# Deformable convolution with a gathered neighbour table: the table built from normalised rows that TensorE turns, as interleaved row pairs

## The reference, cut to what matters

```python
x = x + _L0_conv_ref(_gn(x), offset_w, offset_b, conv_w)      # _gn: group norm, (v - mean) / sqrt(var + eps)

def _L0_conv_ref(x, offset_w, offset_b, conv_w):
    offset = conv2d(x, offset_w) + offset_b                   # 9 taps, 2 coordinates each
    xp = pad(x, 1)                                            # zeros around the normalised image
    p = p0 + pn + offset                                      # where each tap of each pixel samples
    q = floor(p)
    ...
    g_lt = (1 - (py - qlt_y)) * trunc(1 - (px - qlt_x))
    g_rb = (1 - (qrb_y - py)) * trunc(1 - (qrb_x - px))
    g_lb = (1 - (py - qlt_y)) * (1 - (qrb_x - px))
    g_rt = (1 - (qrb_y - py)) * (1 - (px - qlt_x))
    x_off = g_lt * xp[qlt_y, qlt_x] + g_rb * xp[qrb_y, qrb_x] + g_lb * xp[qlt_y, qrb_x] + g_rt * xp[qrb_y, qlt_x]
    return conv2d(x_off, conv_w, stride 3)                    # the 9 samples of a pixel by the 9 taps
```

## Time and profile before

| | |
|---|---|
| median of 3 runs | 3207.58 us (3206.52 to 3216.11) |
| profiled execution | 3214.02 us, its span 3212.2 us |
| TensorE busy | 2880.1 us, 90% |
| VectorE busy | 1898.5 us, 59% |
| ScalarE busy | 1828.8 us, 57% |
| GpSimd busy | 1764.4 us, 55% |
| granted TensorE clock, mean | 0.957 of full speed |
| moved by DMA | 405.97 MB |

### The profile page before, as it was taken

The page is one execution under the profiler, slowest core; times in us unless marked ns, Lnnn a source line. Parts: engine busy times, 40 slices in busy tenths (PEclk is TensorE's granted clock), DMA queues, the critical chain, the costliest instruction groups (busy, mean ns, idle before and its releaser), DMA issues. The chain is left out here.

```text
span 3212.2 us, 53916 instructions
## 1 busy us (share of the span) xinstructions
PE 2880.1 (90%) x19490; PEld 2195.3 (68%) x19490; DVE 1898.5 (59%) x7142; ACT 1828.8 (57%) x4004; POOL 1764.4 (55%) x1815
## 2 busy tenths in 40 slices
PE   4588999999999999999999999999999998999555
PEld 2466776777777777677777776777767776777432
DVE  1456664766576664766477664766486657564324
ACT  1355665666566665666566665666566666664220
POOL 1777764775467654775467644765477556710000
PEclk9699999999999999999999999999999999999787
DMA  5634333552255333643255333633255324411397
GB/s 148 200 112 129 116 112 108 144 139 86 87 153 154 94 96 105 159 119 104 88 136 154 94 90 110 170 110 102 84 148 158 89 81 110 117 66 43 118 341 282
DMA packets 265861, 405.97 MB, mean 126 GB/s; under 512 B 44681, under 2 KB 175977, under 8 KB 265083
## 3 DMA queue, kind: packets, MB, share of 16 engines
q0 software_dynamic: 86400, 236.04, 26.4%
q1 hardware_dynamic: 175323, 153.11, 15.7%
q10 hardware_dynamic: 3872, 13.37, 1.0%
HBM read 368.42 MB, written 85.35 MB: 141 GB/s over the span
## 5 line engine op out<-in xcount | busy, mean ns | idle before, releaser
L495 POOL DMA_INDIRECT shared<-pair_table,idx x1800 | 1752.2, 973 | 1061.5 <-issue 524.6
L1041 PE MATMUL bank_o<-vals,prob_t 128*128 128x128 f32 x5200 | 701.0, 280 | 50.5 <-ACT prob_t L531 49.0
L531 ACT ACTIVATE prob_t<-bank_r 128x512 f32<-128x512 f32 (+3 forms) x728 | 394.9, 547 | 609.6 <-PE bank_r L1028 607.4
L751 DVE CUSTOM_DVE_ANT_0 prob<-bank_s,mask 128x512 f32<-128x512 f32 (+3 forms) x728 | 453.8, 631 | 456.9 <-PE bank_s L1019 453.5
L1041 PEld LDWEIGHTS bank_o<-vals,prob_t 128*128 128x128 f32 x5200 | 637.4, 193 | 84.1 <-ACT prob_t L531 73.7
L1019 PE MATMUL bank_s<-keys,qt 128*128 128x512 f32 (+3 forms) x1456 | 661.4, 560 | 17.4 <-DVE cmax L751 17.4
L518 ACT ACTIVATE shared<-shared,wa 128x128 f32<-128x128 f32 x1800 | 564.2, 390 | 75.9 <-DMA shared<-pair_table,idx 75.9
L741 DVE SCALAR_TENSOR_TENSOR shared<-shared,wb 128x128 f32<-128x128 f32 x1800 | 502.3, 346 | 118.1 <-ACT shared L518 117.4
L1005 PEld LDWEIGHTS bank_conv<-convw_t,smp_t 128*128 128x128 f32 x3600 | 460.1, 200 | 97.8 <-ACT smp_t L524 56.7
L1005 PE MATMUL bank_conv<-convw_t,smp_t 128*128 128x128 f32 x3600 | 497.2, 286 | 32.3 <-ACT smp_t L524 32.2
L1028 PE MATMUL bank_r<-ident,prob 128*128 128x128 f32 x2600 | 417.3, 279 | 1.8 <-ACT prob L598 1.8
(11 more groups left out here) (155 smaller groups left out, 2315.2 us busy)
## 6 DMA issues: line engine op xcount, KB each, us to landing
pair_table<-in_dram SPq DMA_DIRECT2D x224, 224.0 KB
shared<-in_dram SPq DMA_DIRECT2D x32, 1024.0 KB, 9.2
shared<-pair_table,idx POOLq DMA_INDIRECT x1800
shared<-in_dram SPq DMA_DIRECT2D x8, 1568.0 KB
t<-in_dram SPq DMA_DIRECT2D x48, 256.0 KB
t_dram<-t SPq DMA_DIRECT2D x48, 256.0 KB
stage<-t_dram SPq DMA_DIRECT2D x8, 832.0 KB, 6.8
pm_dram<-logit SPq DMA_DIRECT2D x8, 800.0 KB, 6.6
```

The source lines that it names most:

```text
L495: pool.indirect_dma_start(g[t % RING][:, n, :], None, pair_table[b % 2], bass.IndirectOffsetOnAxis(ap=idx[:, b % 2, i * TAPS + n:i * TAPS ...
L531: act.activation(prob_t[q % 2][:, 0:w], ring_bank(("prob", t, c))[:, 0:w], ACT.Copy)\
L751: dve.tensor_tensor_reduce(prob_at(t, k0, w), bank_s[q % 2][:, 0:w], m, 1.0, NEG, ALU.add, ALU.max, cmax[t % 2][:, c:c + 1]).then_inc(scor ...
L1041: last = pe.matmul(attn_ps, prob_t[q % 2][:, n * P:(n + 1) * P], vals[:, slot(tb, at), :], start=(at == 0), stop=(at == ti))
```

## The change

The table is now built from the normalised image. TensorE turns `xpad` in pieces of two image rows (`turn_rows`): for this a row of `xpad` is 64 pixels wide instead of 58, so that two rows are 128 columns. Four such transposes fill a PSUM bank of the ring of three, ScalarE copies the bank (`keep_rows`), and SyncE stores it twice (`store_rows`), once as the upper and once as the lower row of a pair, so that the table holds row y and row y + 1 of each column interleaved. One of its rows is 128 floats; a gather takes two rows from an index on, which is one of the two pairs or the other as the index is even or odd. There are 7 such groups for an image: before the first tile for image 0, in steps 6 to 12 for the next image else. Outside, the table keeps zeros; 8 border writes remain.

Gone are the table copies, `u` with its 9 operations on VectorE and its transpose, `shift` with its matmuls, copy and product, and the scale in the copy of samples. The formulas of the two weights and of the index change with the layout; the index comes last in the chain (step 17 instead of 16).

```diff
-ROWS = 2 * HP * WP
+XW = 64
+BLOCK = 2 * XW
+PLANE = HP * BLOCK
...
+ROW_GROUP = 4
+ROW_GROUPS = H // (2 * ROW_GROUP)
+ROWS_STEP = 6
...
-INDEX = (12, 13, 14, 16, 17, 18)
+INDEX = (12, 13, 14, 16, 17)
...
+def rows_of(step):
+    b, s = divmod(step, TILES)
+    n = s - ROWS_STEP
+    return [(b + 1, n)] if b + 1 < B and 0 <= n < ROW_GROUPS else []
...
-    order = []
+    order = [("rows", 0, n) for n in range(ROW_GROUPS)]
     for step in range(END):
         if step < ALL:
             order += [("smp", step, p) for p in range(PIECES)]
+        order += [("rows", *k) for k in rows_of(step)]
...
+            def store_rows(k, n):
+                at = ROW_GROUPS * k + n
+                after(rows_ev, at + 1)
+                for j, y in ((0, 1 + 2 * ROW_GROUP * n), (1, 2 * ROW_GROUP * n)):
+                    sp.dma_start(cells[k % 2][y * XW:(y + 2 * ROW_GROUP) * XW, j].rearrange("(i p) c -> p i c", p=P),
+                                 rows_out[at % 2][:]).then_inc(rows_stored[at % 2], 16)
...
+            def keep_rows(k, n):
+                at = ROW_GROUPS * k + n
+                after(rows_tp, at + 1)
+                after(rows_stored[at % 2], 32 * (at // 2))
+                act.activation(rows_out[at % 2][:], ring_bank(("rows", k, n))[:].rearrange("p (i c) -> p i c", c=C),
+                               ACT.Copy).then_inc(rows_ev, 1)
...
-                for use in misc_at(step, "E") + misc_at(step, "F"):
+                for use in misc_at(step, "E"):
+                    keep_misc(use)
+                for k, n in rows_of(step):
+                    keep_rows(k, n)
+                for use in misc_at(step, "F"):
                     keep_misc(use)
...
+            def turn_rows(k, n):
+                after(normalised, k + 1)
+                free_ring(("rows", k, n))
+                for i in range(ROW_GROUP):
+                    at = (1 + 2 * (ROW_GROUP * n + i)) * XW
+                    last = pe.transpose(ring_bank(("rows", k, n))[:, i * P:(i + 1) * P], xpad[:, at:at + 2 * XW], ident[:])
+                last.then_inc(rows_tp, 1)
...
-                    if p == PIECES - 1:
-                        after(weighed, b + 1)
-                        last = pe.transpose(bank[:, 3 * P:], u[:, b % 2, i * TAPS:i * TAPS + P], ident[:])
...
-                        emptied(after, ("shift", b, 0))
-                        pe.matmul(conv_ps, smp_t[p][0:TAPS, 3 * P:], shift[:, b % 2, :], start=False, stop=True)\
-                          .then_inc(conv_done, 1)
+                        last.then_inc(conv_done, 1)
```

More of the change, by code:

```diff
@@ L93, in misc_order @@
 def misc_order():
-    order = [("gstat", 0, 0), ("shift", 0, 0)]
+    order = [("gstat", 0, 0)]
     for c in range(OFF_CHUNKS):
@@ L101, in misc_order @@
         for place in "EFML":
-            order += [u for u in misc_at(step, place) if u[0] not in ("gstat", "shift", "chunk", "turn") or u[1] > 0]
+            order += [u for u in misc_at(step, place) if u[0] not in ("gstat", "chunk", "turn") or u[1] > 0]
     return order
@@ L280, in first_part @@
              for r in range(RING)]
-        smp_t = [sb(f"smp_t{p}", [P, (3 if p < PIECES - 1 else 4) * P]) for p in range(PIECES)]
+        smp_t = [sb(f"smp_t{p}", [P, 3 * P]) for p in range(PIECES)]
+        rows_out = [sb(f"rows_out{r}", [P, ROW_GROUP, C]) for r in range(2)]
         t1 = sb("t1", [P, T1_GROUPS * PER, C])
@@ L323, in first_part @@
         x_in = sem("x_in")
-        table_in = [sem(f"table_in{r}") for r in range(2)]
+        rows_stored = [sem(f"rows_stored{r}") for r in range(2)]
         gathered = [sem(f"gathered{r}") for r in range(RING)]
@@ L490, in _ @@
                 after(indexed, b + 1)
-                after(table_in[b % 2], 16 * 4 * (H // TABLE_ROWS) * (b // 2 + 1))
+                for r in range(2):
+                    after(rows_stored[r], 32 * len(range(r, ROW_GROUPS * (b + 1), 2)))
                 after(smp_tp, PIECES * (t - RING + 1))
@@ L538, in keep_misc @@
                 filled(after, use)
-                if what == "shift":
-                    last = act.activation(shift[:, b % 2, :], bank_misc[0:TAPS, 0:P], ACT.Copy,
-                                          scale=inv_rs[0:TAPS, b % 2:b % 2 + 1])
-                elif what == "chunk":
+                if what == "chunk":
                     last = act.activation(offs[:, n % 2 * OFF_W:(n % 2 + 1) * OFF_W], bank_misc[:, 0:OFF_W], ACT.Copy)
@@ L570, in keep_misc @@
                 last.then_inc(misc_ev_a, 1)
-            after(zeroed, 8)
+            after(zeroed, 6)
             after(setup_mm, 1)
@@ L583, in _ @@
             normalise(0)
-            for use in MISC_ORDER[:MISC_AT["turn", 0, 3] + 1]:
-                keep_misc(use)
+            for c in range(OFF_CHUNKS):
+                keep_misc(("chunk", 0, c))
+                keep_rows(0, c)
             for p in range(PIECES):
@@ L915, in fill_misc @@
                     last = pe.matmul(bank_misc[:, 0:2], group[:], mv_x[:], start=True, stop=True)
-                elif what == "shift":
-                    after(affine_done, b + 1)
-                    for k in range(TAPS):
-                        last = pe.matmul(bank_misc[0:TAPS, 0:P], nb[:, TAPS - 1 - k:2 * TAPS - 1 - k],
-                                         convw_t[:, k, :], start=(k == 0), stop=(k == TAPS - 1))
                 elif what == "chunk":
                     after(normalised, b + 1)
-                    rows = xpad[:].rearrange("p (y x) -> p y x", x=WP)
+                    rows = xpad[:].rearrange("p (y x) -> p y x", x=XW)
                     for k in range(TAPS):
@@ L978, in _ @@
               .then_inc(setup_mm, 1)
-            after(zeroed, 8)
+            after(zeroed, 6)
             after(setup_ev, 4 + TAPS)
-            for use in MISC_ORDER[:MISC_AT["turn", 0, 3] + 1]:
-                fill_misc(use)
+            fill_misc(("gstat", 0, 0))
+            for c in range(OFF_CHUNKS):
+                fill_misc(("chunk", 0, c))
+                turn_rows(0, c)
+                if c % 2 or c == OFF_CHUNKS - 1:
+                    fill_misc(("turn", 0, c // 2))
             for step in range(END):
@@ L1052, in _ @@
                     fill_misc(use)
+                for k, n in rows_of(step):
+                    turn_rows(k, n)
                 if step < ALL:
```

154 lines of the change are left out of this document (61 added, 93 removed), and 2 rows, old and new, of the table MISC.

## The result

The changed kernel takes 3108.72 us (median of four runs, 3104.21 to 3111.21) where the kernel before takes 3207.05 us beside it (3205.88 to 3216.11): a ratio of 0.9686, 95% interval 0.9665 to 0.9707. The forecast was 3107 us. The changed kernel run again later gave 0.9689 (0.9669 to 0.9708). So the number was right. The working was right in part: two of its terms, what the products covered and the clock, were off by 3 us an image or so, in opposite directions.

What follows compares the result with a forecast made beforehand. It took TensorE to bound images 1 to 7 and gathers the start. Savings of 3.5 us in image 0, 84.3 in images 1 to 6 and 13.2 in image 7 sum to 101, forecasting 3107 us, range 3075 to 3142.

Steps and rivals of the forecast that it cites:

- The shift product: TensorE, each of 200 tiles: removing the 9-row product was to save 0.51 us a tile.
- the page's rule: Trainium skill: few contraction rows take as long as 128; would price the shift product at 0.22 us, against the timeline's 0.51.
- The transpose of summed weights: TensorE, each tile, before the scores: removing this transpose was to save 0.11 us.
- The cover: Loss where the removed shift product had hidden ScalarE's copy of turned probabilities: 0.3 us an image, at worst 3.6.
- rival A: Steps 7 to 18 swallow the gain, the shift product being cover throughout: 43 us of it, 3150 us; chance 0.11.
- its mark: Sign that short steps swallow the gain: TensorE's waits on the probabilities' copy grow from 4.0 to over 9 us an image.
- The clock: TensorE's granted clock, 0.98 to 1.00 in middle images, was to stay; bounds 42 us more gained or 50 given back.
- Making the shift: TensorE, once an image: removing the 18 records that make the shift was to save 2.3 us.
- the row turns: TensorE: 28 added transposes of image rows, for seven of the images, were to cost 3.05 us an image.
- The start: Before the first gather: chunks 1.5 us earlier, index chain 2.6 longer, statistics 0.4; +1.5 us in sum, bounds -1 to +8.
- Image 7, 13.2: Last image, with no next one to prepare: 15.5 us saved less 2.3 for tiles already waiting for VectorE, 13.2 us.
- rival D: GpSimd writes one descriptor per table row, so a gather's 0.95 us doubles: some 4400 us in all; chance 0.03.

Runs made afterwards that it cites:

- experiments 1 and 2: Changed kernel with one more product a tile where the shift product stood: with 9 rows 4314.83 us (0.9911 of before), with 128 rows 4303.72 us (0.9881), on slower chips.
- experiment 3: Changed kernel with a tenth transpose of samples a tile put back, its result unread: 0.9875 of the kernel before, on a slower chip.
- experiment 10: Faster chip: changed kernel again 0.9689; with ScalarE's scalings reordered 0.9661; last, with that order and chunk products moved early in steps 5 and 6, 0.9564 (3066.36 us).
- experiment 8: Kernel before with the shift made for image 0 only and used for all images: 4255.94 us for 4291.9, 0.9921, on a slower chip.
- experiment 4: Changed kernel with the table built for image 0 only, row transposes, copies and stores of images 1 to 7 left out: 0.975, on a slower chip.
- experiment 9: The changed kernel itself, unaltered, beside the kernel before on a slower chip: 4206.07 us for 4293.57, 0.9779.

## Why the prediction was right, and where it was not

- **The shift product, 0.51 us: right, and shown** (experiments 1 and 2: 0.508). Of the page's rule and the row, the row held. A filled step gives 0.67 and not 0.62, since the transposes behind the product were slow too.
- **The transpose of summed weights, 0.11 us: right, and shown** (experiment 3: 0.109, by the trace).
- **The cover, forecast 0.3 us an image in all: the step of the prediction that failed.** The prediction looked at the first copy of turned probabilities in a long step, which lies under TensorE's work, and took that to hold for the steps with two and three chunks too. There the second copy, not the first, ends last, behind nine scalings; in steps 12, 13 and 15 to 18 the distance across it is the same with and without the product (4.39 us in the last four), and each of steps 15 to 18 gave 0.11 us (the transpose) and not 0.62. Six times 0.51 is 3.1 us an image. Steps 13 to 18 gave 1.3 us for 3.7, steps 7 to 12 none for 0.6: 3 us an image lost. It is rival A's mechanism in six of its twelve steps, so at half of its price: the wait for the copy grew from 4.0 to 7.4 us an image, and its mark was 9. The prediction's case against A ("the product stands before them") read the place of the wait and not the engine that set it.
- **The clock, forecast unchanged: failed the other way.** In steps 5 and 6, at their two waits, the clock fell to the lower level in six of six images before and in three of six now. Against forecast terms of 2.9 us these two steps gave 6.4; in image 1, at a granted clock of 0.96 in both kernels, they gave 2.9 (46.3 and 43.4 us), the forecast. So some 3.5 us an image, 21 in all, is the clock. The last kernel of experiment 10 shows that on this chip the falls go with these waits: with both shortened there is none. Why the unchanged waits come with fewer falls in the changed kernel stays open in part; experiment 8 points to the making of the shift, which stood between the two waits, since without it alone the clock in these steps was higher.
- **Making the shift, 2.3 us, and the row turns, 3.05: consistent, the turns not isolated.** Step 5 with one fall of the clock in each kernel (image 1) gave 27.7 - 25.0 = 2.7 us where 0.62 + 2.3 - 0.1 = 2.8 was worked out, and experiment 8 gives some 2.4 for the shift, roughly; experiment 4 was too coarse for the turns.
- **The start, forecast +1.5: it was +4.7.** The longer chain cost 2.3 us (the prediction has 2.6; six more operations at its 0.41 are 2.5), but four chunk products ran at some 4 us where the prediction's sum left them as they were; that was inside its bounds of -1 to +8. Its signs were missed by this: the first gather at 86.20 us for 82 to 84, tile 16 at 289.4 for 287. With it, image 0 gave 1.1 us for 3.5.
- **Image 7, 13.2: measured 9.3**, most likely by the same loss of cover: its waits for the copy are 10.6 us, where before they were 6.9. These missing 4 us were hidden by the 6.8 us by which the end of this execution was shorter.
- **GpSimd's gathers (rival D): fell.** 970 ns for 973.

Against the 101 us of the sum the profiled executions differ by 105.7: -18 for cover in steps 7 to 18, -3 for steps 2 and 3, -2.4 for image 0 and -4 for image 7, +21 for the clock, +5 for the filled steps and step 19, +7 at the end (rounded, together to within 1 us). The medians differ by 98.3. The forecast of 3107 is right to 2 us by this balance, which is luck; the range is right because its bounds held both errors.

## What to carry to other kernels

Before an instruction is priced at its own length, find for each kind of step which engine sets the distance across it: where two copies of another engine with work between them span it, as in six steps of an image here, what TensorE does inside is free, and taking it out gains nothing. Removing such a wait by moving that other work helps only if the work isn't needed as early elsewhere; giving TensorE something to do during the wait, when the next image's products are at hand, did help, by 4.6 us an image here. And in a kernel that falls to the lower clock behind waits of 2 to 3 us, leave room in the forecast for both signs: here the clock was a fifth of the gain.

## What the runs showed of the hardware that was not expected

- A float32 product with 9 rows of contraction by 128 columns took 0.508 us of TensorE's time, one with 128 rows 0.223, and the four transposes behind the 9-row one 0.49 us for 0.43 to 0.44.
- On some chips the same program takes 1.34 times as long, 4291.9 us for 3207. In experiment 9 ScalarE and VectorE are as long busy as on the other chip (1793.1 and 1899.1 us for 1782.7 and 1895.6), and waits between engines end late, by some 2 us in the rows shown. From the last tile's samples to the end it takes 336.5 us there, no more than on the other chip.
- On the faster chips, two waits of 2.1 to 2.2 and 2.8 us in an image came with a lower clock in six of six images of the kernel before and in three of six of the changed one; with 0.7 and 0.4 us there was none in 2256 us.
